# A decoder layer in float32: copies of turned probabilities, two mask casts and the spread of the shared key on ScalarE in place of VectorE

## The reference

```
x = layernorm(x + attention(x))        # 16 heads of 128, 4 key heads, rotary, window
x = layernorm(x + long_conv(ctx, ctx, x))   # per head: conv(k_i * v_j) times q_i, summed over i
x = layernorm(x + ffn(x)):
    gating = softmax(x @ W_gate.T);  idx = argmax(gating);  indicator = one_hot(idx, 16)
    q, k, v = split(x @ W_qkv.T, 3)
    k_shared = einsum('bth,bthd->btd', indicator, k)      # one key head per token
    v_shared = einsum('bth,bthd->btd', indicator * max(gating), v)
    att = softmax(causal(q @ k_shared.T / sqrt(16)))      # 16 query heads share that key
    y = att @ v_shared
```

## Time and profile before

| | |
|---|---|
| median of 3 runs | 341.36 us (340.34 to 342.01) |
| the profiled execution's own time | 341.08 us |
| its span, first to last instruction | 339.2 us |
| busy: TensorE / its loads | 320.3 us (94%) / 246.6 us (73%) |
| busy: VectorE / ScalarE / GpSimd | 255.6 (75%) / 232.2 (68%) / 198.2 us (58%) |
| share of the chain that ended last | TensorE 76%, VectorE 9%, GpSimd 7%, issue 3%, ScalarE 3%, DMA 2% |
| granted TensorE clock, mean over the span | 0.986 |

### The profile page before, as it was taken

The page is one execution under the profiler, slowest core; times in us unless marked ns, Lnnn a source line. Parts: engine busy times, 40 slices in busy tenths (PEclk is TensorE's granted clock), DMA queues, the critical chain, the costliest instruction groups (busy, mean ns, idle before and its releaser), DMA issues.

```text
span 339.2 us, 6308 instructions
## 1 busy us (share of the span) xinstructions
PE 320.3 (94%) x2102; PEld 246.6 (73%) x2102; DVE 255.6 (75%) x507; ACT 232.2 (68%) x692; POOL 198.2 (58%) x284
## 2 busy tenths in 40 slices
PE   7968999999999999999999999999789999999982
PEld 2747888888888888888888888665366666666641
DVE  2784886775886884786784785999977899998645
ACT  3639877868777777777867866521448787778781
POOL 0488763665763665773674772799791767912112
PEclk9989999999999999999999999999979999999998
DMA  7931010031010021110012000000000000000010
GB/s 244 338 130 45 20 34 0 1 107 53 30 31 2 1 85 52 51 33 0 2 52 83 3 0 2 1 1 2 0 1 2 2 15 3 16 18 17 1 33 31
DMA packets 5616, 13.08 MB, mean 39 GB/s; under 512 B 848, under 2 KB 3024, under 8 KB 5328
## 3 DMA queue, kind: packets, MB, share of 16 engines
q1 hardware_dynamic: 5040, 11.90, 10.3%
q10 hardware_dynamic: 544, 0.79, 0.8%
HBM read 11.63 MB, written 1.05 MB: 37 GB/s over the span
## 4 chain that ended last, share of the span: by engine, by line
PE 76%; DVE 9%; POOL 7%; issue 3%; ACT 3%; DMA 2%; POOLq 0%; DVEq 0%
PE bank L371 18%; PE bank L512 12%; PE bank L402 8%; PE bank L388 7%; PE bank L479 4%; PE bank L665 4%; PE bank L676 4%; PE bank L631 3%; POOL q_rope L315 3%; PE bank L501 3%; PE bank L686 2%; POOL q_rope L318 2%; PE bank L496 2%; PE bank L498 2%; DMA w_raw<-in_wqkv 2%
## 5 line engine op out<-in xcount | busy, mean ns | idle before, releaser
L1526 POOL TENSOR_TENSOR t_sin<-rot,sin 128x512 f32<-128x512 f32 x40 | 51.2, 1285 | 27.1 <-ACT rot L831 21.7
L1548 POOL TENSOR_TENSOR prob<-prob,rden 128x512 f32<-128x512 f32 x32 | 33.6, 1050 | 46.7 <-DVE rden L1151 46.7
L864 ACT ACTIVATE prob<-bank,neg_max 128x128 f32<-128x128 f32 x128 | 45.3, 374 | 0.2
L512 PE MATMUL bank<-wo_hi,head_hi 128*128 128x256 f32 x128 | 38.3, 299 | 0.4 <-DVE head_lo L1203 0.4
L402 PEld LDWEIGHTS bank<-k_rope,q_rope 128*128 128x128 f32 x256 | 34.3, 197 | 5.8 <-DVE q_rope L1101 3.1
L1000 ACT ACTIVATE prob<-bank,fneg_max 128x128 f32<-128x128 f32 x128 | 36.7, 380 | 2.2 <-DVE fneg_max L1382 2.2
L402 PE MATMUL bank<-k_rope,q_rope 128*128 128x128 f32 x256 | 34.8, 280 | 2.6 <-DVE q_rope L1101 2.6
L1088 DVE TENSOR_TENSOR t_cos<-bank,cos 128x512 f32<-128x512 f32 x40 | 27.4, 687 | 11.5 <-ACT rot L831 10.7
L512 PE MATMUL bank<-wo_lo,head_hi 128*128 128x256 f32 x128 | 36.0, 281 | 0.0
L512 PE MATMUL bank<-wo_hi,head_lo 128*128 128x256 f32 x128 | 36.0, 281 | 0.0
L1516 POOL TENSOR_TENSOR kv<-ctxT 128x256 f32<-128x256 f32 (+3 forms) x64 | 35.9, 591 | 0.0
(11 more groups left out here) (126 smaller groups left out, 806.0 us busy)
## 6 DMA issues: line engine op xcount, KB each, us to landing
w_raw<-in_wqkv SPq DMA_DIRECT2D x3, 768.0 KB, 4.8
toep<-in_toep SPq DMA_DIRECT2D x8, 256.0 KB, 3.0
wo_raw<-in_wo SPq DMA_DIRECT2D x4, 512.0 KB, 3.4
x_raw<-in_xt SPq DMA_DIRECT2D x2, 512.0 KB, 5.8
ctxT<-in_ctx SPq DMA_DIRECT2D x1, 1024.0 KB, 9.1
x<-in_x SPq DMA_DIRECT2D x1, 1024.0 KB, 9.8
out<-x SPq DMA_DIRECT2D x8, 128.0 KB, 1.7
wf<-in_wf SPq DMA_DIRECT2D x1, 784.0 KB, 4.6
```

Source lines behind the costliest of these rows:

```text
L512: last = pe.matmul(acc_bank[k // 2][:, (k % 2) * D:(k % 2 + 1) * D], hp[:, k % 2, h * P:(h + 1) * P], wp[:, v % 2, h, :], start=(h + n == ...
L864: last = act.activation(prob[:, k % 2, h * P:(h + 1) * P], score_bank[k % 2][:, h * P:(h + 1) * P], ACT.Exp, bias=neg_max[:, k % 2, h:h + ...
L1526: pool.tensor_tensor(t_sin[:, par, :].rearrange("p (b t) -> p b t", b=BH), rot[:, par, :].rearrange("p (b t) -> p b t", b=BH), sin[:, :].u ...
L1548: pool.tensor_tensor(own, own, rden[:, k % 2, :].unsqueeze(2).to_broadcast([P, HG, P]), ALU.mult).then_inc(norm_done, 1)
```

## The change

ScalarE takes over from VectorE: the first three copies of turned probabilities of the last unit (the fourth was there already), the casts of the causal mask and of the identity to bf16, and, for each of the eight blocks of phase B, the spread of the shared key into `krep` (new function `keys_in`). TensorE, GpSimd and SyncE keep their lists. The computation is the same.

```diff
-            def last_prob_copy():
-                t = 4 * UNITS - 1
+            def last_prob_copy(k):
+                t = 4 * (UNITS - 1) + k
                 act.wait_ge(pt_done, t + 1)
                 act.wait_ge(pv_done, t - 1)
-                act.copy(probT[:, 1, :], probT_bank[:, :]).then_inc(ptcopy_done, 1)
+                act.copy(probT[:, k % 2, :], probT_bank[:, :]).then_inc(ptcopy_done, 1)
...
                 if not has_next:
                     item("C1")
+                    last_prob_copy(0)
                     item("C2")
                     item("C3")
                     head_copy(0)
+                    last_prob_copy(1)
                     mix_query(0, 0)
                     exps(u, 2)
                     exps(u, 3)
                     head_copy(1)
                     mix_query(1, 1)
+                    last_prob_copy(2)
+                    act.wait_ge(in_ffn, 48)
+                    act.wait_ge(in_ident, 16)
+                    act.copy(causal[:, :], causal_raw[:, :])
+                    act.copy(identb[:, :], ident[:, :]).then_inc(mask_done, 1)
                     head_copy(2)
-                    last_prob_copy()
+                    last_prob_copy(3)
...
+            def keys_in(b):
+                act.wait_ge(shared_done, b + 1)
+                act.wait_ge(const_set, 1)
+                at_least(act, ksT_done, b, 1)
+                act.copy(kz, kv_shared[:, 0, :].unsqueeze(1).unsqueeze(1).to_broadcast([P, 2, FC, FD])
+                         ).then_inc(krep_done, 1)
...
             query_copy(0, 0)
+            keys_in(0)
             values_in(0)
...
                 if 1 <= i + 1 < NB:
+                    keys_in(i + 1)
                     values_in(i + 1)
                     key_copy(i + 1, (i + 1) % 2)
...
                     first_stats(0)
-                    prob_copy(0)
                     row_max(u, 2)
                     first_apply(0, 0)
                     first_apply(1, 1)
-                    prob_copy(1)
                     head_low(0)
...
                     head_low(1)
-                    prob_copy(2)
...
                     dve.wait_ge(in_ffn, 48)
-                    dve.tensor_copy(causal[:, :], causal_raw[:, :])
-                    dve.tensor_copy(identb[:, :], ident[:, :]).then_inc(mask_done, 1)
                     gating(0)
...
                 dve.tensor_reduce(kv_shared[:, :, :], kv_masked[:, :, :, :], axis=AX.X, op=ALU.add).then_inc(shared_done, 1)
-                dve.wait_ge(shared_done, b + 1)
-                at_least(dve, ksT_done, b, 1)
-                dve.tensor_copy(kz, kv_shared[:, 0, :].unsqueeze(1).unsqueeze(1).to_broadcast([P, 2, FC, FD])
-                                ).then_inc(krep_done, 1)
```

## The result

The changed kernel takes 345.65 us (median of 20 runs, 343.53 and up), against 341.34 us (20 runs) before: a ratio of 1.0114, 95% interval 1.0081 to 1.0146. (The ratio leaves out the slow runs, up to 626.71 us.) The forecast was 342.3 us with a range from 340.3 to 343.8. The sign was right, the size was not: 4.3 us slower instead of 0.9.

A forecast was written before the change was run, and what follows sets the result against it. TensorE was taken to bound phase B's steps, VectorE to be busiest at the passage from phase A. Steps 1.6 us lost less passage 0.66 gained gave 0.94 slower: 342.0 for the profiled execution, 342.3 as median, range 340.3 to 343.8.

The forecast's parts named there:

- Copies and casts: Last unit: moving three copies off VectorE gains 0.1 us, between -0.22 and 0.28; the casts change nothing.
- First gating: Passage from phase A to B: without the casts `gneg` starts 0.17 us earlier; gain 0.2 us, between 0 and 0.29.
- First spread, TensorE's part: Passage, block 0: TensorE no longer waits for the spread that VectorE took 2.08 us over; 0.36 us gained.
- the passage: From phase A to phase B: copies, gating and first spread together gain 0.66 us, between 0.14 and 0.93.
- Steps: Phase B, steps 1 to 6: ScalarE's spread behind the yT copy delays loading `krep`; 1.6 us lost, about 1.1 to 2.5.
- VectorE's other 1.6 us are not passed on: Passage, first spread: the rest of VectorE's saved time gains nothing, as its next work waits for TensorE's scores.
- the sign that the prediction named for itself: Prediction is wrong if the steps' wait is missing, the spread exceeds 0.45 us, or the passage returns over 1.1 or nothing.
- Slower: Rival, steps: ScalarE's eight-piece stride-0 spread costs more than a flat copy; at 0.55 us each, 343.6 us; chance 0.2.
- Not late: Rival, steps: ScalarE's spread starts sooner or TensorE makes good the late load; only the passage remains, 340.7 us; chance 0.15.
- Faster: Rival, first spread: VectorE's whole 1.85 us reaches the end and the steps lose nothing; 339.5 us; chance 0.08.

The follow-up runs named there:

- experiment 3: The kernel before with only the three copies and the two casts on ScalarE, all spreads on VectorE; 341.23 us, ratio 1.0008.
- experiment 2: The kernel before with only the spreads of blocks 1 to 7 on ScalarE; 344.05 us, ratio 1.0051 (profiled execution 342.40 us).
- experiment 7: The changed kernel with GpSimd's products for block 3 waiting for block 1's norm, and ScalarE's spread ahead of the yT copy; 342.39 us, ratio 1.0037.
- experiment 1: The kernel before with only the spread of block 0 on ScalarE; 342.65 us, ratio 1.0042.
- experiment 4: The changed kernel with GpSimd's products for block 3 waiting until VectorE has written the norm of block 1; 342.94 us, ratio 1.0027.
- experiment 6: The changed kernel with seven fillers on TensorE ahead of the `x2_turn` of block 2; 344.34 us, ratio 1.0073.
- experiment 9: The kernel before with spreads of blocks 1 to 7 on ScalarE and GpSimd's products for block 3 waiting for block 1's norm; 343.53 us, ratio 1.0053.
- 5: The kernel before, GpSimd stopping within its products for block 2 until VectorE has spread the key of block 0; 340.80 us, ratio 0.9992.
- 11: A second profile, without edit, of the kernel before with only the spreads of blocks 1 to 7 on ScalarE; 344.38 us.
- 10: A second profile of the changed kernel, without edit; 343.85 us.

## Why the prediction was wrong, by its own steps

- **Copies and casts: right.** Forecast a gain of 0.1; `x2_turn` of block 0 came 0.16 earlier relative to the row above it (0.19 in experiment 3's profile), and experiment 3's median shows no difference.
- **First gating: wrong, but small.** Forecast 0.2. `gneg` started at 230.26, 0.11 behind the end of the gate copy (230.15): the forecast had left out that hand-over, and against the turn ahead it gained 0.06 us instead of 0.17. `gscore` then lasted 0.83 us beside GpSimd's products (0.78 in the earlier trace rows), and the turn behind it stood 0.62 later than before, as the one ahead of it. Nothing came through.
- **First spread, TensorE's part: right.** Forecast 0.36, got 0.43 between the two turns, without a wait. Up to that turn the passage gave 0.59 us, and the sum had 0.66; that this came so close is in part luck, since the gating gave nothing and the other two terms a little more than was forecast.
- **Steps: right in place and kind, a little large.** Forecast 1.6, measured 1.26 in experiment 2. The copy took 0.30, not 0.33, and the hand-over 0.05, not 0.08. The reason that I gave, the place behind the copy of yT, is not enough: experiment 7 moved the spread ahead of that copy and won 0.03 us a step.
- **The step that failed: "VectorE's other 1.6 us are not passed on: its next work waits for TensorE's scores."** That was true of the row maxima and false of what stands ahead of them. Between the spread and the maxima lies the norm of block 1, which waits only for GpSimd's power. It moved up from 238.79 to 238.02 and took 3.20 us instead of 0.82: TensorE's `x2_turn` of block 1 lost 1.43 us that no term of the sum had. Experiment 1 shows it without the rest of the change, and experiment 4, which takes the hold-up away, gets back about 2.8 us. It is also the sign that the prediction named for itself: the passage gave nothing back. The prediction had the very effect in its hands, since it read the 2.08 us of the first spread as a hold-up by GpSimd, but asked only who would be rid of it, not which instruction would stand there next.
- **The clock: not in the sum at all.** The forecast took a granted clock of 1.00 behind the passage. In the profiled execution `x2_turn` to `key_turn` of block 2 took 1.7 us more with the fall at 256 to 260 than without it (experiment 6), less 0.8 that the shorter first fall gave back. It isn't in every run: the profile of 343.85 us is without it. What decides whether it comes is open: with the added wait it is absent from experiment 4's profile (whose twelve runs lie between 342.15 and 343.25) and present in experiment 9's.
- **The rivals.** "Slower" had the right sign for a wrong reason: the eight-piece copy from a stride-0 source costs 0.30 us, below the point of 0.46 from which that rival would have decided. "Not late" fell with the 0.33 us of idle time in each step. "Faster" fell with the norm of block 1: what VectorE got back never reached the end.

The sum of the profiled execution, in us: 0.78 (between executions) - 0.16 - 0.43 + 1.43 - 0.16 + 1.92 (clock 1.7, step 0.2) + 0.99 = 4.37, of the 4.4 between the two spans. It explains these two executions; that the medians lie 4.3 apart for the same reasons is inferred, not shown, since the 0.78 and the second fall change from run to run.

Not settled: why the norm of block 1 gets through in 0.8 us beside the products in some kernels. It begins 0.06 to 0.09 us behind the first product in all of them. It lasted 0.81 or 0.82 in the kernel before and in experiments 2, 3, 5 and 11, where VectorE makes the first spread, and 3.20 in the kernel after and experiments 1, 6 and 10, where ScalarE does. The split is clean, its mechanism was not tested.

## What to carry to other kernels

When work is taken off an engine, look up which of its next instructions moves, and beside whose work it will then stand: if the instruction removed was being held up, the next one of the same kind inherits the hold-up. A sum whose terms are all right can still miss a wait that changes its place. And a profile is one execution: before a term is read from it, a second profile of the same kernel shows which of its gaps and clock falls come back.

## What the runs showed of the hardware

A VectorE instruction from SBUF to SBUF in f32 can be held through a whole series of GpSimd's f32 products, not only for one of them: the spread took 2.08 us beside six products' ends and 0.23 once they waited (experiment 5), the norm 3.20 beside five products and 0.41 once they waited (experiment 4), and in experiment 7 another norm took 2.03 from 252.68, to 0.15 behind the end of GpSimd's set (254.56). The Trainium skill ("SBUF — State Buffer", "SBUF: two separate sides") says that whoever starts first gets the pair of ports for the whole instruction and the other is blocked. It leaves open who gets the pair next when the following GpSimd instruction stands ready, and this case's traces show both outcomes: the holds above go on over several products, while the norm of 0.82 us (238.79 in the kernel before) ends beside the second product. The reduction to `t_cos`, 2048 elements from SBUF, is not stretched: 2.27 us beside GpSimd's products (231.85 in the kernel after) and 2.27 with GpSimd idle (255.83 in experiment 7).

The granted clock of the same program went two ways over the same instructions (experiments 2 and 11), with 2 us between the two times. Medians can't be compared to a fraction of a per cent without asking how the runs are spread.
